# A third PSUM bank for the scores of the row maxima, and denominators in the ring of the transposed scores

## The reference, cut to what matters

```
qkv = x @ Wqkv;  k, v = compress(k), compress(v);  k, v = [null_k; k], [null_v; v]
dots = einsum('bhid,bhjd->bhij', q, k) * d ** (-0.5)
dots = where(q_idx < k_idx, mask_value, dots)
attn = softmax(dots, axis=-1)
out  = einsum('bhij,bhjd->bhid', attn, v)
```

## Time and profile before

| | us |
|---|---|
| median of 3 runs | 5562.23 (5559.91 to 5567.71) |
| the profiled execution, its time | 5570.41 |
| the profiled execution, its span | 5568.7 |
| stage b in it, from about 766 to about 2606 | 1840 |
| PE busy over the span | 5418.1 (97%) |

### The profile page before, as it was taken

How to read it: one execution, slowest core, us unless ns; L and a number is a source line. 1 busy time by engine, 2 the same in 40 slices (tenths; PEclk the granted TensorE clock), 3 DMA queues, 4 the chain that set the end, 5 groups by cost and what they waited for, 6 DMA issues and landing times. The chain is left out here.

```text
span 5568.7 us, 102394 instructions
## 1 busy us (share of the span) xinstructions
PE 5418.1 (97%) x32880; PEld 4532.0 (81%) x32880; DVE 3938.2 (71%) x8367; ACT 2584.3 (46%) x3737; POOL 2995.3 (54%) x2620
## 2 busy tenths in 40 slices
PE   8999989999999999998999999999999999999999
PEld 7888866666666666665999999999999999999886
DVE  7777767777777777776766666666666666666656
ACT  3222223333334333333666666666666666666510
POOL 2222213565555555311677777777777777777514
PEclk9999989999999999999999999999999999999999
DMA  6555554344444444443667677677787667676648
GB/s 218 180 182 182 175 158 126 113 134 120 122 130 119 138 115 122 122 129 106 126 112 158 134 144 157 134 156 165 171 210 178 134 128 164 134 155 112 159 174 283
DMA packets 475957, 832.21 MB, mean 149 GB/s; under 512 B 56212, under 2 KB 157317, under 8 KB 473102
## 3 DMA queue, kind: packets, MB, share of 16 engines
q1 hardware_dynamic: 334862, 537.99, 30.2%
q0 software_dynamic: 140928, 292.13, 28.7%
HBM read 499.48 MB, written 330.47 MB: 149 GB/s over the span
## 5 line engine op out<-in xcount | busy, mean ns | idle before, releaser
L1717 POOL DMA_INDIRECT mid_base<-e_rows,e_ox x556 | 1176.7, 2116 | 371.7 <-POOL e_ox L1712 210.2
L1828 DVE TENSOR_TENSOR e_wgu_lo<-e_wgu,e_wgu_hi 128x2048 fp32r<-128x2048 f32 x278 | 637.4, 2293 | 805.1 <-ACT e_wgu_hi L1751 633.5
L1705 POOL DMA_INDIRECT e_xg<-mid_xn,e_ix x556 | 621.3, 1118 | 338.7 <-POOL e_ix L1702 228.7
L1764 ACT CAST e_xT_hi<-e_ps_t 128x512 fp32r<-128x512 f32 x556 | 299.2, 590 | 936.6 <-PE e_ps_t L1894 936.6
L1017 POOL DMA_INDIRECT mid_ids<-b_pairs,b_cell x512 | 610.4, 1192 | 148.9 <-issue 147.9
L1907 PE MATMUL e_ps_g<-e_xT_hi,e_wgu_hi 128*128 128x256 f32 x2224 | 652.7, 293 | 1.7 <-DVE e_gated L1845 1.7
L1907 PE MATMUL e_ps_g<-e_xT_lo,e_wgu_hi 128*128 128x256 f32 x2224 | 629.7, 283 | 0.0
L1907 PE MATMUL e_ps_g<-e_xT_hi,e_wgu_lo 128*128 128x256 f32 x2224 | 629.4, 283 | 0.0
L1907 PE MATMUL e_ps_u<-e_xT_hi,e_wgu_hi 128*128 128x256 f32 x2224 | 629.4, 283 | 0.0
L1907 PE MATMUL e_ps_u<-e_xT_lo,e_wgu_hi 128*128 128x256 f32 x2224 | 629.4, 283 | 0.0
L1907 PE MATMUL e_ps_u<-e_xT_hi,e_wgu_lo 128*128 128x256 f32 x2224 | 629.4, 283 | 0.0
(11 more groups left out here) (303 smaller groups left out, 13520.4 us busy)
## 6 DMA issues: line engine op xcount, KB each, us to landing
b_xT_hi<-mid_xT_hi SPq DMA_DIRECT2D x32, 1024.0 KB
b_xT_lo<-mid_xT_lo SPq DMA_DIRECT2D x32, 1024.0 KB
mid_base<-b_x SPq DMA_DIRECT2D x32, 1024.0 KB
e_wgu<-in_gate_w SPq DMA_DIRECT2D x62, 512.0 KB
e_wgu<-in_up_w SPq DMA_DIRECT2D x62, 512.0 KB
e_wd<-in_down_w SPq DMA_DIRECT2D x62, 512.0 KB
ec_cell<-mid_base SPq DMA_DIRECT2D x88, 256.0 KB, 5.0
b_q<-mid_q_hi SPq DMA_DIRECT2D x84, 256.0 KB
```

Source lines behind the costliest of these rows:

```text
L1705: pool.indirect_dma_start(xg[s][:, i, :], None, t["xn"], bass.IndirectOffsetOnAxis(ap=ix[s][:, i:i + 1], axis=0))\
L1717: pool.indirect_dma_start(t[f"base{i}"], bass.IndirectOffsetOnAxis(ap=ox[s][:, i:i + 1], axis=0), rows[s][:, i, :], None, compute_op=ALU.a ...
L1764: act.copy(xT_hi[s][:, i * DC // 2 * RB:(i + 1) * DC // 2 * RB], ps_t[i][:, :]).then_inc(xT_hi_ready, 1)
L1828: dve.tensor_tensor(wgu_lo[s][:, :], wgu[s][:, :], wgu_hi[s][:, :].bitcast(F32), ALU.subtract)\
```

## The change

The scores' ring gets a third bank; `ps_d` is gone. Entry j of the scores' ring (17 for a unit) now uses bank j % 3 and waits for entry j - 3. The denominators become an entry of the ring `ps_t`: after the second transposed score of the following unit, or, for a unit with n = 0, after its own null scores. The denominators of n = 0 move from slot 7 to slot 11, and `normalise` of such a unit moves on DVE from slot 1 of the next unit to the very start of its slot 0.

```diff
-        ps_s = [ps(f"ps_s{r}", [P, 512]) for r in range(2)]
+        ps_s = [ps(f"ps_s{r}", [P, 512]) for r in range(3)]
         ps_t = [ps(f"ps_t{r}", [P, 512]) for r in range(2)]
         ps_o = ps("ps_o", [P, 512])
-        ps_d = ps("ps_d", [P, 512])
...
         def ring_before(u, i):
-            if i >= 2:
-                return s_emptied, 16 * u + i - 1
-            if u == 0:
+            v, e = divmod(17 * u + i - 3, 17)
+            if v < 0:
                 return None
-            return (s_emptied, 16 * u) if (17 * u + i) % 2 == (17 * u - 2) % 2 else (mt_emptied, u)
+            return (mt_emptied, v + 1) if e == 16 else (s_emptied, 16 * v + e + 1)
 
         def s_bank(u, i):
-            return ps_s[(17 * u + i) % 2]
+            return ps_s[(17 * u + i) % 3]
+
+        def t_order():
+            for u in range(NU):
+                first, null = t_first(u), t_null(u)
+                for i in range(first, null + 1):
+                    if i == first + 2 and u and (u - 1) % NCH:
+                        yield "sum", u - 1
+                    yield "scores", i
+                if u % NCH == 0:
+                    yield "sum", u
+            yield "sum", NU - 1
...
+        def t_before(kind, i):
+
+            at = t_place[kind, i]
+            if at < 2:
+                return None
+            before, e = t_ring[at - 2]
+            return (den_ready if before == "sum" else t_emptied), e + 1
...
+                    if k == 0 and u and (u - 1) % NCH == 0:
+                        normalise(u - 1)
...
-                    if k == 1 and u:
+                    if k == 1 and u and (u - 1) % NCH:
                         normalise(u - 1)
...
-                if i >= 2:
-                    pe.wait_ge(t_emptied, i - 1)
+                before = t_before("scores", i)
+                if before:
+                    pe.wait_ge(*before)
...
-                if u:
-                    pe.wait_ge(od_emptied, u)
+                pe.wait_ge(*t_before("sum", u))
                 src = p_sum if n else p_diag
                 for h in range(HPC):
-                    last = pe.matmul(ps_d[h * DH:(h + 1) * DH, :], ones[:, :], src[:, h, :], start=True, stop=True)
+                    last = pe.matmul(t_bank("sum", u)[h * DH:(h + 1) * DH, :], ones[:, :], src[:, h, :], start=True, stop=True)
...
-                    if k == 7 and n == 0:
-                        denominators(u)
...
+                    if k == 11 and n == 0:
+                        denominators(u)
```

More of the change, by code:

```diff
@@ L846, in ring_before, with t_bank @@
         def ring_before(u, i):
-            if i >= 2:
-                return s_emptied, 16 * u + i - 1
-            if u == 0:
+            v, e = divmod(17 * u + i - 3, 17)
+            if v < 0:
                 return None
-            return (s_emptied, 16 * u) if (17 * u + i) % 2 == (17 * u - 2) % 2 else (mt_emptied, u)
+            return (mt_emptied, v + 1) if e == 16 else (s_emptied, 16 * v + e + 1)
         def s_bank(u, i):
-            return ps_s[(17 * u + i) % 2]
+            return ps_s[(17 * u + i) % 3]
[9 more added lines that the diff above has]
+            yield "sum", NU - 1
+        t_ring = list(t_order())
+        t_place = {entry: at for at, entry in enumerate(t_ring)}
+        def t_bank(kind, i):
+            return ps_t[t_place[kind, i] % 2]
+        def t_before(kind, i):
[4 more added lines that the diff above has]
+            return (den_ready if before == "sum" else t_emptied), e + 1
         def steps(u):
@@ L1065, in exponent @@
                         act.wait_ge(dve_summed, c - 1)
-                act.activation(dst[:, h, :], ps_t[i % 2][:, :], ACT.Exp, scale=SCALE).then_inc(t_emptied, 1)
+                act.activation(dst[:, h, :], t_bank("scores", i)[:, :], ACT.Exp, scale=SCALE).then_inc(t_emptied, 1)
             pv_of_past = [pv_index(u, kt) for u in range(NU) for kt in range(u % NCH)]
@@ L1074, in null_exponent @@
                     act.wait_ge(od_emptied, u)
-                act.activation(p_null[:, :], ps_t[i % 2][:, :], ACT.Exp, scale=SCALE).then_inc(t_emptied, 1)
+                act.activation(p_null[:, :], t_bank("scores", i)[:, :], ACT.Exp, scale=SCALE).then_inc(t_emptied, 1)
             def half_tanh(s, j):
@@ L1187, in normalise @@
                     dve.wait_ge(att_ready, u)
-                dve.tensor_tensor(den[:, :], ps_d[:, :], p_null[:, :], ALU.add).then_inc(den_ready, 1)
+                dve.tensor_tensor(den[:, :], t_bank("sum", u)[:, :], p_null[:, :], ALU.add).then_inc(den_ready, 1)
                 dve.scalar_tensor_tensor(o[:, :], p_null[:, :], nullv[:, c:c + 1], ps_o[:, :], ALU.mult, ALU.add)\
@@ L1386, in turn_max @@
                 pe.wait_ge(nm_ready, u + 1)
-                pe.wait_ge(s_emptied, 16 * u + 15)
+                pe.wait_ge(*ring_before(u, 16))
                 for qt in range(QTC):
@@ L1393, in scores_t @@
                 g, i = u // NCH, t_index(u, kt, h)
-                if i >= 2:
-                    pe.wait_ge(t_emptied, i - 1)
+                before = t_before("scores", i)
+                if before:
+                    pe.wait_ge(*before)
                 if kt == u % NCH and h == 0:
                     pe.wait_ge(mt_emptied, u + 1)
-                pe.matmul(ps_t[i % 2][:, :], kc[g % 2][:, h, 2 + kt * P:2 + (kt + 1) * P], q[u % 3][0:KM, h, :], start=True,
+                pe.matmul(t_bank("scores", i)[:, :], kc[g % 2][:, h, 2 + kt * P:2 + (kt + 1) * P], q[u % 3][0:KM, h, :], start=True,
                           stop=True).then_inc(t_filled, 1)
@@ L1402, in scores_null @@
                 i = t_null(u)
-                pe.wait_ge(t_emptied, i - 1)
-                pe.matmul(ps_t[i % 2][:, :], null_heads[:, :], q[u % 3][:, 0, :], start=True, stop=True).then_inc(t_filled, 1)
+                pe.wait_ge(*t_before("scores", i))
+                pe.matmul(t_bank("scores", i)[:, :], null_heads[:, :], q[u % 3][:, 0, :], start=True, stop=True).then_inc(t_filled, 1)
             def values(u, kt):
```

## The result

The changed kernel takes 5568.8 us (median of 20 runs, 5560.4 to 5584.9), the kernel before 5561.5 in the same comparison (20 runs). The ratio is 1.0016, 95% interval 1.0008 to 1.0023: 7 to 9 us slower, inside the 0.2% that I had called no change, 23 us above the 5546 that I had forecast. The profiled executions differ by as much, 5577.1 against 5570.4 us. Of these 6.7 us, 4.4 lie in stage b; the other 2.3 lie in front of it and behind it, in code that the change leaves alone.

What follows compares the result with a forecast made beforehand. PE, busy 97% of the span, was taken as the bound, with DVE in some slots. Terms 2 - 1 + 8 - 21 - 3 - 1 = -16 us gave 5554 profiled, 5546 median; 8-in-10 range 5515 to 5579.

Steps and rivals of the forecast that it cites:

- (a): Slot 0 of 47 units: denominators wait for the first exponent to free their bank, 0.52 us each, +24.4 us.
- (b): Slot 5, third bank: waits for row maxima shorten by 0.38 us at n = 0 and 0.71 at n = 2.
- (c): Units with n = 1: earlier `normalise` and third bank gain 1.8 us in each of twelve disturbed units, -21 us.
- the pause goes with the instruction: Rival, n = 1 units: pauses stay on `hT` and row maxima; only the bank gains, 5561 us; chance 0.22.
- Coupled rings: Rival, disturbed units: PE depends on `normalise`, first row maximum comes 1.26 us later; 5576 us; chance 0.15.
- (d): Disturbed n = 2 units, slot 0: new wait is a later one moved forward, -1 us for twelve.
- the clock swings: Rival: the 47 new gaps lower PE's clock, some 1.8 us each, +84; half gives about 5590; chance 0.04.
- (e): Counted at nothing: n = 0 denominators in slot 11 instead of 7, hidden `normalise`, moved `max_rows` wait, DMAs unchanged.
- The rule on the clock: Skill's rule that small idle gaps between matmul groups can swing the clock, making the 47 new gaps dangerous.
- my terms of undisturbed units: Per undisturbed unit: n = 0 +0.14 us, n = 1 about 0.7 gained, n = 2 -0.2, n = 3 +0.52.
- The chance of 0.48 for faster: Whole kernel: chance 0.48 of being faster by over 0.2%, below 5551 us.

## Why the prediction was wrong

**(a), the new wait: right place, size too small.** 0.61 us a unit instead of 0.52, since the release took 0.11 us and not the 0.05 that I chose from a range of 0.05 to 0.11, and 0.03 came behind it. At 47 units that is 4 us. That it is paid in full, nothing being given back, is shown by the sum moved between the scores and by the variant without ring waits.

**(b), the bank at the end of a burst: right at n = 0, twice too large at n = 2.** 0.38 against 0.38 and 0.33 against 0.71. At n = 2 slot 5 gains 0.51 us and slot 7 loses some 0.1 to 0.3: DVE carries part of the work over.

**(c), units with n = 1: mechanism right, size too large.** Its first steps are in the rows of unit 25 above; that DVE's chain is ahead from there shows in slots 2 to 5, 1.08 us shorter. The gain was 1.37 us a disturbed unit and not 1.8, in all -19.7 us and not -24. A part of it is the clock: it fell in five of these units before and in four now, and the four units that had 1.00 in both traces (5, 13, 25, 37) gained 1.26 us each. The rival that the pause goes with the instruction had its chain untouched and a gain of 0.5; the trace speaks against it. *Coupled rings* wanted the first row maximum later than 0.5 us after today's; in the mean of the twelve units it starts 5.85 us into the unit, before 5.99.

**(d), disturbed units with n = 2: the step that failed.** "I take the new wait as one of those moved forward; I count -1 us." It was +9.7 in twelve units, and n = 2 as a whole missed by 12.6 of the 20 us between -16 and +4.4. The wait itself came as forecast: the load of the denominators, 2.4 to 2.6 us into the unit before, stood at 3.5 to 5.0, and I had worked out 4.9. That later waits would give it back was right too, where the clock stayed up: in the six units at 1.00 slot 0 is 1.4 us longer, slots 1, 2, 4 and 5 together 2.1 shorter and slot 7 0.4 longer, -0.29 us a unit. What (d) put at nothing is TensorE's clock. PE had worked on through slot 0 while the others stood; now it stands there itself, 2.32 to 2.40 us in seven units and 0.96 to 1.59 in five. Behind the longer gaps the clock fell in six of seven cases, behind the shorter ones never. PE's busy time in the windows, for the same matmuls, is 29.1 us at 1.00, 30.4 at 0.95 and 31.8 at 0.90 on average, which makes 10.6 us in the six units, the whole of the +9.7.

The prediction had looked at the clock for the 47 gaps as a rival, *the clock swings* (0.04), and set it aside because "no gap below 2.4 us in the rows shown lowered the clock". The rest of the same trace held two cases against that: units 17 and 49 of the kernel before lost the clock behind gaps of 1.7 and 2.0 us on PE. The bound that I had kept for (d) (+12, "no later wait absorbs it") came near the truth by luck, since its reason is not what happened. All this is read from two traces; no experiment met the pause, and why unit 22 kept its clock behind 2.32 us stays open.

**(e), at nothing: right in sum, not in parts.** The denominators of n = 0 in slot 11 cost 0.18 us a unit (2.9 in 16), and the moves at n = 1 give 2.7 back.

**The rule on the clock.** In the undisturbed units 56, 58 and 59 above the new gaps stood at a granted clock of 1.00, the upper level, and without the pause all 47 did. The Trainium skill ("TensorE: Matmul & The Clock Gate", section "A second HAM failure mode: psum-queue depth-cycling") would have such gaps make the clock swing; these did not. The gaps that the pause had stretched to 2.3 us did, in six units: between unit 2 and the end of stage b the lower level took 23.8 us in five places before and 40.8 us in ten with the change.

**Without the pause** my terms of undisturbed units, 16 x (0.14 - 0.7 - 0.2 + 0.52), make -4 us, and the measurement is +13.4: n = 2 misses by 8 of these 17 us, n = 0 and n = 1 by 4 each. So the size of the bank at n = 2 is there what the clock is in the first traces. The chance of 0.48 for faster hung on the one large gain that I had found, in a disturbance that comes and goes.

## What to carry to other kernels

A ring of banks is not only a matter of how many: what counts is who filled the bank just ahead of the new user. A tile that joins a ring of two directly behind two fills waits for the reader of the first of them, in each round; one place earlier, or in a ring whose entry of that moment was emptied long ago, it waits for nothing. When a wait is to be moved into a stall of the other engines, it is not enough that later waits give its time back: here they did, and the loss came from the clock, which fell behind six of the seven gaps of 2.3 to 2.4 us that PE now had there. So read the granted clock unit by unit, before and after. And for each step that is made later, follow its result through every queue to the loads that stand behind it in program order, since that cost 170 us here.

## What was not expected of the hardware

- **The pause.** In the first two traces ACT, DVE and SP went on only some us after PE's work that they wait for (`hT` 5.97 us idle) in the 12 units of n = 1 and the 12 of n = 2 between the scatters; in the nine traces of the other runs with scatters, two of them of the same programs, they did not, and the kernel before took 5500 us and not 5561. The units with n = 1 and n = 2 are 43.7 + 27.0 = 70.7 us shorter there in the kernel before. Whether it is the chip or its state, and what in it, stays open.
- **The clock behind short gaps.** With the same gap on PE, 2.32 and 2.34 us, unit 22 kept the upper level and unit 38 fell to the lower one for 6.8 us; unit 9 of the changed kernel (n = 1) kept it behind 2.97 us. So the length of the gap alone does not decide it. The 47 gaps at the new wait, 0.54 us each on PE, never lowered it without the pause.
- **DVE beside GpSimd.** Without the pause, in 8 of the 12 units 5 to 49 of the kernel before, the subtraction `hT_lo` took 1.9 to 2.3 us, without scatters never over 1.31 and in the first traces not over 1.32. Unit 25 of the kernel before, with scatters and then without, and GpSimd in the first of them:

```profile
1476.46 1.94 DVE L1212 TENSOR_TENSOR b_hT_lo<-b_hT,b_hT_hi 128x512 fp32r<-128x512 f32 x1
...
1475.54 2.31 POOL L1010 TENSOR_SCALAR_AFFINE_SELECT b_p_diag<-b_p_diag 128x512 f32<-128x512 f32 x4
```

```profile
1470.85 0.93 DVE L1209 TENSOR_TENSOR b_hT_lo<-b_hT,b_hT_hi 128x512 fp32r<-128x512 f32 x1
```

  DVE is on the path in these slots (119.22 of 119.22 us busy in slots 2 to 5), so the 1.0 us is paid. The scatters delay GpSimd's four selects until they run in one piece under the subtraction, which ends within 0.6 us of them (1478.40 against 1477.85). The Trainium skill ("SBUF — State Buffer", "Who interferes with whom") has the two engines share a pair of ports under an exclusive lock, and a DVE instruction with two inputs in SBUF contend with a GpSimd instruction that reads SBUF. The traces agree: in the second kernel two selects ran beside it, from 1470.63 for 1.63 us, and it took 0.93; beside no GpSimd work it took 0.7 in all of the 51 and 81 places of these two traces, beside scatters alone 0.7 as well, and beside three or four selects 1.9 to 2.3. With `normalise` two slots later and the loads first, the selects fall elsewhere: 0.7 in all twelve of these units, and 1.5 to 1.6 beside three selects in seven others. No run holds the selects away from it on purpose, so the lock itself is not told from another cause.
- **A late store.** Moving `normalise` by two slots cost 170 us through a queue that neither engine of the move waits in.
